# Attention steps of a conv and attention chain: scores of both images first, then the values, then the maxima tiles, on TensorE

## The chip, the cores and the metric

One Trainium2 chip, one core of it. The metric is the device time in microseconds (us) of one execution of the whole program; the median of several executions counts. TensorE (PE) multiplies, VectorE (DVE) reduces, ScalarE (ACT) takes exponentials, GpSimd (POOL) adds, SyncE (SP) issues the transfers. All five run their own list of instructions and meet only at semaphores.

## The reference

Four layers on an input of 8 images, 64 channels, 56 by 56 pixels; each layer adds its result to x. The first three (a dynamic filter, a gate, a convolution with ternary weights) are not touched by the change. The fourth is attention over all 3136 pixels of an image:

```python
def _L3_conv_ref(x, q_w, k_w, v_w):
    xf = x.reshape(b, din, hw)
    Q = jnp.einsum('kc,bcp->bkp', q_w, xf)
    K = jnp.einsum('kc,bcp->bkp', k_w, xf)
    V = jnp.einsum('vc,bcp->bvp', v_w, xf)
    S = jnp.einsum('bkp,bkq->bpq', Q, K)
    A = jax.nn.softmax(S, axis=-1)
    z = jnp.einsum('bpq,bvq->bvp', A, V)
...
x = x + _L3_conv_ref(_gn(x), L3_conv_q_w, L3_conv_k_w, L3_conv_v_w)
```

## The kernel before, in words

The images are taken in four groups of two. The two images of a group lie one above the other in the 128 partitions, and in attention each is called h (0 or 1). The first three layers of all groups run first, for 574 us; then comes attention for all groups, and it is what the change touches.

**Superblocks and steps.** Attention goes over 28 superblocks (seven per group, each 448 queries of both images), and each superblock over 25 steps j (128 keys each, the last one 64 keys). A running number k = 25 * superblock + j counts the steps. One step of PE, written out in `superblock` of the PE program, has these parts:

- `values(j)` (L1418): the exponentials of step k, in one of five slots of `Pb`, times V, added into the output bank. It is float32: four matmul records.
- `scores(k + 2, h)` (L1391): the scores of the step after the next, for image h, into the pair of PSUM banks that step k has used. So the exponentials of step k must be done before (`exp_done`). Two records for an image, one for each half of the 64-column halves of the array. The last of them releases ACT (`st_ready`).
- `max_tile` (L1353): scores again, for queries of the next superblock, whose maxima must be known before that superblock starts. 49 tiles a superblock, spread by a plan made ahead: two in nearly every step, one in step 2, and three in most steps of the first superblock up to step 17. Three PSUM banks (4, 5, 7) go round among them. Two records a tile.
- in step 2 also `denominators` (L1401, L1405) of the superblock before.

A matmul that uses 64 of the 128 columns occupies one half of the array, and each pair of records fills both halves. In step 22 (it makes the scores of the 64-key step 24) the scores of both images use the same half, so that half runs 0.38 us behind the other until the next wait that holds both. Below it is called the slow half.

**The other engines.** ACT takes the exponentials of step k (L1015) when `st_ready` says that the scores are there; then, after those of step k, it sums the exponentials of the tiles of step k - 2 that belong to the first three of seven query blocks (L980, "summed" tiles), for which it needs DVE's maxima. After the exponentials of step 0 it copies the finished output of the superblock before (`copy_output`, L1004), which waits for `pv_done`, the end of the values of step 24. DVE takes the maxima of each tile (L752) in the order in which PE makes them; in step 3 it turns the denominators (L801), between the two tiles of step 3 it inverts them (L806), between those of step 4 it turns them back (L811), after step 17 it splits the maxima in three parts (L767 to L790). Then SP sends the parts as rows into the queries (L407); `mrow_loaded` tells PE in step 23. POOL adds up the exponentials (L1145).

**What a tile waits for.** Before a tile PE waits until its bank is free (`wait_bank`): for DVE's maxima of the tile that had the bank (`max_bank_free`), or for ACT's sum (`max_scores_summed`), or, for the bank of the denominators, for DVE's transpose of them (`reciprocal_step`). By the plan the second tile of a step waits in 279 steps of the later superblocks for the second tile of the step just before, and in 308 for the first tile of it; the first tile of a step waits for something two steps back, nearly always.

**The order that is changed.** The order within a step is written by hand in the loop over j: values, then scores of image 0, a tile, scores of image 1, the other tile. Step 0 of each superblock already has the order scores, scores, values, tiles, since its values wait for `copy_output` (`ocopy`).

Of the kernel before, what the change touches and what calls it, by code (L numbers as in the profile page):

```python
# [41 lines left out]
NQ = -(-HW // QC)  # L42
# [3 lines left out]
SBS = NJ * GROUPS  # L46
# [20 lines left out]
ROW_LOADS = 4  # L67
# [99 lines left out]
def build(nc, x, weights, vectors, cst, out):  # L167
    with ExitStack() as ctx:
# [3 lines left out]
        def sem(name):  # L172
            return ctx.enter_context(nc.semaphore(name))
# [180 lines left out]
        mrow_loaded = sem("max_rows_loaded")  # L354
# [815 lines left out]
        def _(pe):  # L1170
# [176 lines left out]
            def attention():  # L1347

                def tile_of(bank, target, b, t):

                    g, s = divmod(target, NJ)
                    for h in range(2):
                        last = mm(PS[C * h:C * h + C, bank, 0:CH],  # L1353
                                  Qs[g % 2][0:KROWS, h, s * CH + b * C:s * CH + b * C + C],
                                  Ks[g % 2][0:KROWS, h, t * CH:(t + 1) * CH], start=True, stop=True)
                    return last

                def wait_rows(g):
                    pe.wait_ge(k_loaded, 16 * SPREADS * (g + 1))
                    pe.wait_ge(q_loaded, 16 * SPREADS * (g + 1))  # L1360

                def wait_bank(last):

                    what, count = last
                    if what == "reduced":
                        pe.wait_ge(mx_free, count)
                    elif what == "summed":
                        pe.wait_ge(mx_summed, count)
                    elif what == "transposed":
                        pe.wait_ge(rstep, count)  # L1370

                def max_tile(target, i, _, __, bank, last):
                    if i == 0 and target % NJ == 0:
                        wait_rows(target // NJ)
                    wait_bank(last)
                    tile_of(bank, target, *ORDER[i]).then_inc(mx_ready, 1)
# [9 lines left out]
                def scores(k, h):  # L1386

                    j = k % NQ
                    g, s = divmod(k // NQ, NJ)
                    for c in range(0, key_rows(j), C):  # L1390
                        ins = mm(PS[c:c + C, 2 * (k % 2) + h, 0:CH], Ks[g % 2][0:KROWS + 3, h, j * QC + c:j * QC + c + C],  # L1391
                                 Qs[g % 2][0:KROWS + 3, h, s * CH:(s + 1) * CH], start=True, stop=True)
                    if h == 1:
                        ins.then_inc(st_ready, 1)

                def denominators(sidx, bank):

                    pe.wait_ge(dcol_ready, sidx + 1)
                    for b in range(ACT_BLOCKS):
                        for h in range(2):  # L1400
                            mm(PS[C * h:C * h + C, bank, b * C:(b + 1) * C], dcol[:, b:b + 1].to_broadcast([P, C]),  # L1401
                               identf[:, C * h:C * h + C], start=True, stop=True)
                    pe.wait_ge(psum_pool, POOL_SUMS * (sidx + 2))
                    for h in range(2):
                        last = mm(PS[C * h:C * h + C, bank, REST:CH], ones[:, :], accP[:, h, REST:CH], start=True, stop=True)  # L1405
                    last.then_inc(d_ready, 1)

                def superblock(sidx):

                    V = Vs[sidx // NJ % 2]  # L1410

                    def values(j):
                        if j == 0:
                            pe.wait_ge(ocopy, sidx + 1)
                            if sidx % NJ == 0:
                                pe.wait_ge(v_loaded, 16 * (sidx // NJ + 1))
                        for h in range(2):
                            last = mm(PS[C * h:C * h + C, OB, 0:CH], V[:, j, C * h:C * h + C],  # L1418
                                      Pb[:, j % PSLOTS, h, :], start=(j == 0), stop=(j == NQ - 1))
                        last.then_inc(pv_done, 1)  # L1420

                    for j in range(NQ):
                        k = NQ * sidx + j
                        tiles = list(TILES_AT.get(k, ()))
                        pe.wait_ge(exp_done, k + 1)
                        if j:
                            values(j)
                        for h in range(2):
                            if k + 2 < NQ * SBS:
                                if j == NQ - 2 and h == 0:  # L1430
                                    pe.wait_ge(mrow_loaded, 16 * ROW_LOADS * (sidx + 1))
                                scores(k + 2, h)
                            if tiles and j:
                                max_tile(*tiles.pop(0))
                        if not j:
                            values(j)
                        for tile in tiles:
                            max_tile(*tile)
                        if j == FINISH_STEP - 1 and sidx:
                            bank, last = DEN_BANK.get(sidx - 1, (7, ("nothing", 0)))  # L1440
                            wait_bank(last)
                            denominators(sidx - 1, bank)
# [22 lines left out]
                for sidx in range(SBS):  # L1465
                    superblock(sidx)
# [82 lines left out]
```

## Time and profile before

| | us |
|---|---|
| median of 3 runs | 1672.35 |
| lowest and highest | 1670.41 and 1673.25 |
| the profiled execution, its own time | 1674.61 |
| its span, first to last instruction | 1672.8 |
| PE busy in the span | 1611.8 (96%) |
| ACT busy | 1194.7 (71%) |
| DVE busy | 1210.8 (72%) |
| POOL busy | 1111.8 (66%) |
| chain that ended last: share of PE | 83% |

The profiled execution spends 1.8 us outside its span. Shares over the whole span mix the first three layers with attention. In a row of the timeline the first number is the start in us from the start of the span, the second the duration in us from the first start to the last end of the merged records; "PEld" is the loading of weights, which runs beside the matmuls. A merged row of values with x4 and 0.92 us covers 0.75 us of PE, since the record of a matmul is longer than the time after which the next can start.

### The profile page before, as it was taken

The page shows a single profiled execution, that of the slowest core. Times are in us where ns is not written, and L with a number is a line of the kernel's source. Part 1 is how long each engine was busy: PE and PEld are TensorE (multiplying, and loading weights), DVE is VectorE, ACT ScalarE, POOL GpSimd, SP SyncE. Part 2 cuts the span into 40 slices and gives each one's busy share as a digit, 9 for nine tenths or more (in the row PEclk, how much of TensorE's full clock was granted, in tenths as well). Part 3 has the DMA queues.
Part 4 walks back from the last instruction along what each step waited for, and adds up shares of the span by engine and source line. Part 5 has one row for each costly group of instructions (what it writes and reads, how often), then busy time and mean ns, then how long its engine had stood idle before and what let it go on. Part 6 is the DMA issues. An engine that isn't in the chain of part 4 may idle for free.

```text
span 1672.8 us, 29841 instructions
## 1 busy us (share of the span) xinstructions
PE 1611.8 (96%) x11035; PEld 865.6 (52%) x11035; DVE 1210.8 (72%) x2322; ACT 1194.7 (71%) x2276; POOL 1111.8 (66%) x886
## 2 busy tenths in 40 slices
PE   5999999999999899999999999999999999999996
PEld 4457457557556245555555555555555555555542
DVE  5865865865955787777777777777777777777750
ACT  2053143144243689999999999999999999999984
POOL 1720730630632168888888888888888888888887
PEclk9999999999999699999999999999999999999998
DMA  2000210210205303200000500000320000000000
GB/s 96 2 38 39 69 39 39 69 39 39 69 7 103 134 2 57 65 14 17 12 13 12 110 13 18 13 12 13 52 69 12 18 12 13 12 7 7 7 7 12
DMA packets 15586, 57.68 MB, mean 34 GB/s; under 512 B 4688, under 2 KB 10960, under 8 KB 13008
## 3 DMA queue, kind: packets, MB, share of 16 engines
q1 hardware_dynamic: 15440, 55.77, 12.5%
q8 instruction: 86, 1.41, 0.3%
q14 instruction: 60, 0.49, 0.1%
HBM read 31.41 MB, written 24.22 MB: 33 GB/s over the span
## 4 chain that ended last, share of the span: by engine, by line
PE 83%; DVE 8%; POOL 5%; issue 2%; ACT 2%; DMA 0%; POOLq 0%; DVEq 0%; ACTq 0%
PE PS L1418 29%; PE PS L1353 15%; PE PS L1391 14%; PE PS L1289 7%; PE PS L1244 5%; PE PS L1232 3%; POOL accP L1145 2%; DVE nmt L752 2%; PE PS L1341 1%; PE PS L1333 1%; DVE nmt L759 1%; PE PS L1279 1%; PE PS L1278 1%; PE PS L1198 1%; DVE st L507 1%
## 5 line engine op out<-in xcount | busy, mean ns | idle before, releaser
L752 DVE TENSOR_REDUCE nmt<-PS 128x1 f32<-128x448 f32 x1323 | 767.2, 617 | 223.2 <-PE PS L1353 222.6
L1145 POOL TENSOR_TENSOR accP<-accP,Pb 128x512 f32<-128x512 f32 (+1 forms) x532 | 674.5, 1268 | 93.5 <-ACT Pb L1015 37.9
L1015 ACT ACTIVATE Pb<-PS 128x896 f32<-128x896 f32 (+1 forms) x700 | 637.0, 915 | 80.1 <-PE PS L1391 69.8
L980 ACT ACTIVATE PS<-PS,nmt 128x448 f32<-128x448 f32 x588 | 356.4, 606 | 16.4 <-DVE nmt L759 9.6
L1418 PE MATMUL PS<-Pb,VT 128*64 128x448 f32 x1400 | 335.9, 541 | 1.9 <-ACT Pb L1015 1.5
L1418 PE MATMUL PS<-Pb,xnf 128*64 128x448 f32 x1400 | 336.4, 540 | 0.0
L1353 PE MATMUL PS<-xnp,xin 96*64 96x448 bf16 x1408 | 265.4, 371 | 7.9 <-ACT PS L980 3.6
L1353 PE MATMUL PS<-Ka,Qa 96*64 96x448 bf16 x1372 | 258.8, 353 | 0.9
L1391 PE MATMUL PS<-xin,xnp 99*64 99x448 bf16 x1372 | 256.3, 353 | 0.8 <-ACT Pb L1015 0.6
L1391 PE MATMUL PS<-Qa,Ka 99*64 99x448 bf16 x1372 | 251.8, 353 | 0.0
L1353 PEld LDWEIGHTS PS<-xnp,xin 96*64 96x64 bf16 x1408 | 87.7, 113 | 138.5 <-issue 61.9
L1353 PEld LDWEIGHTS PS<-Ka,Qa 96*64 96x64 bf16 x1372 | 86.7, 110 | 117.7 <-issue 66.3
L1391 PEld LDWEIGHTS PS<-Qa,Ka 99*64 99x64 bf16 x1372 | 87.5, 109 | 113.0 <-issue 86.4
L1391 PEld LDWEIGHTS PS<-xin,xnp 99*64 99x64 bf16 x1372 | 87.2, 109 | 108.3 <-issue 78.6
L1418 PEld LDWEIGHTS PS<-Pb,VT 128*64 128x64 f32 x1400 | 101.4, 137 | 49.1 <-ACT Pb L1015 14.1
L1418 PEld LDWEIGHTS PS<-Pb,xnf 128*64 128x64 f32 x1400 | 104.5, 137 | 39.9 <-ACT Pb L1015 2.9
L980 ACT ACTIVATION_READ_ACCUMULATOR PS<-PS,nmt 128x1 f32 x588 | 117.1, 199 | 0.0
L1145 POOL TENSOR_TENSOR accQ<-accQ,Pb 128x512 f32<-128x512 f32 x84 | 106.7, 1271 | 13.7 <-ACT Pb L1015 1.9
L614 DVE SCALAR_TENSOR_TENSOR Pb<-PS,cf,xnp 128x896 f32<-128x896 f32 (+1 forms) x80 | 79.3, 1029 | 22.1 <-PE PS L1232 21.5
L1138 POOL TENSOR_TENSOR accQ<-Pb 128x512 f32<-128x512 f32 x28 | 35.6, 1271 | 87.3 <-ACT Pb L1015 87.3
L880 ACT ACTIVATE xnp<-xw,nb,rstd 128x448 f32<-128x448 f32 x28 | 19.9, 751 | 93.5 <-DVE nb L522 93.5
L1244 PE MATMUL PS<-Pb,cs 128*128 128x448 f32 x168 | 76.5, 573 | 9.3 <-DVE xw L627 9.3
(160 smaller groups left out, 1810.0 us busy)
## 6 DMA issues: line engine op xcount, KB each, us to landing
saved_v<-VT SPq DMA_DIRECT2D x4, 1600.0 KB, 11.3
xin<-in_x SPq DMA_DIRECT2D x4, 1568.0 KB, 6.5
saved_x<-xw SPq DMA_DIRECT2D x4, 1568.0 KB, 5.6
out<-xw SPq DMA_DIRECT2D x28, 224.0 KB, 1.9
saved_parts<-parts SPq DMA_DIRECT2D x4, 1176.0 KB, 8.0
xw<-saved_x SPq DMA_DIRECT2D x21, 224.0 KB, 2.6
xnf<-saved_v SPq DMA_DIRECT2D x2, 1600.0 KB, 16.6
VT<-saved_v SPq DMA_DIRECT2D x2, 1600.0 KB, 18.3
```

The source lines that it names most:

```text
L614: nc.vector.scalar_tensor_tensor(out=prod[t][:, 0:m, :].rearrange("p h (r w) -> p h r w", w=W), in0=PS[:, b:b + m, 0:CH].rearrange("p h (r ...
L752: nc.vector.reduce_max(nmt[:, target % 2, b, t:t + 1], PS[0:BLK, bank, 0:CH], X, negate=True).then_inc(mx_free, 1)
L980: return nc.scalar.activation(PS[0:BLK, bank, 0:CH], PS[0:BLK, bank, 0:CH], ACT.Exp, bias=nmt[:, target % 2, b, t:t + 1], accum_out=sm[:, ...
L1015: nc.scalar.activation(Pb[0:r, j % PSLOTS, :, :], PS[0:r, 2 * (k % 2):2 * (k % 2) + 2, 0:CH], ACT.Exp).then_inc(exp_done, 1)
L1138: nc.gpsimd.tensor_tensor(accQ[:, :, REST:CH], Pb[:, 0, :, REST:CH], Pb[:, 1, :, REST:CH], ALU.add).then_inc(psum_pool, 2)
L1145: nc.gpsimd.tensor_tensor((accQ if j < TO_ACCP else accP)[0:r, :, REST:CH], (accQ if j <= TO_ACCP else accP)[0:r, :, REST:CH], Pb[0:r, j % ...
L1232: last = mm(PS[:, 2 * ((TAPS * u + t) % TAP_SLOTS) + i, 0:CH], selb[:, t, :], SF[:, j * CH:(j + 1) * CH], start=True, stop=True)
L1244: last = mm(PS[:, ACCB + i, 0:CH], identf, prod[t][:, i, :], start=(t == 0), stop=(t == TAPS - 1))
L1289: last = mm(PS[:, CONV_BANKS[j % 5], 0:CH], wt[:, t * P:(t + 1) * P], pad_rows_at(src, j * (ROWS * PW) + (t // 3) * PW + t % 3, ROWS), sta ...
L1353: last = mm(PS[C * h:C * h + C, bank, 0:CH], Qs[g % 2][0:KROWS, h, s * CH + b * C:s * CH + b * C + C], Ks[g % 2][0:KROWS, h, t * CH:(t + 1 ...
L1391: ins = mm(PS[c:c + C, 2 * (k % 2) + h, 0:CH], Ks[g % 2][0:KROWS + 3, h, j * QC + c:j * QC + c + C], Qs[g % 2][0:KROWS + 3, h, s * CH:(s + ...
L1418: last = mm(PS[C * h:C * h + C, OB, 0:CH], V[:, j, C * h:C * h + C], Pb[:, j % PSLOTS, h, :], start=(j == 0), stop=(j == NQ - 1))
```

## The change: what it does

In the steps 1 to 24 of a superblock PE's list is put in another order; step 0 stays as it was. Scores of image 0 and of image 1 come first, one behind the other, then the values, then all tiles of the step. Two waits move with this: that for `exp_done` stays first in the step but now stands before the scores, and that for the maxima rows (`mrow_loaded`, step 23) now stands before the values and not behind them. Nothing is added and nothing is removed; the lists of ACT, DVE, POOL and SP are the same as before.

```diff
                         pe.wait_ge(exp_done, k + 1)
-                        if j:
-                            values(j)
-                        for h in range(2):
-                            if k + 2 < NQ * SBS:
-                                if j == NQ - 2 and h == 0:
-                                    pe.wait_ge(mrow_loaded, 16 * ROW_LOADS * (sidx + 1))
+                        if k + 2 < NQ * SBS:
+                            if j == NQ - 2:
+                                pe.wait_ge(mrow_loaded, 16 * ROW_LOADS * (sidx + 1))
+                            for h in range(2):
                                 scores(k + 2, h)
-                            if tiles and j:
-                                max_tile(*tiles.pop(0))
-                        if not j:
-                            values(j)
+                        values(j)
                         for tile in tiles:
                             max_tile(*tile)
```

PE's list before, at the turn from one superblock to the next: step 24, then step 0 up to its values. L1418 are values, L1391 scores, L1353 tiles; one row of values or tiles is one image.

```order
L1418 MATMUL PS<-Pb,VT 64x448 [waits exp_done]
L1418 MATMUL PS<-Pb,VT 64x448
L1391 MATMUL PS<-Qa,Ka 64x448 x2
L1353 MATMUL PS<-Ka,Qa 64x448 [waits max_scores_summed]
L1353 MATMUL PS<-Ka,Qa 64x448
L1391 MATMUL PS<-Qa,Ka 64x448 x2
L1353 MATMUL PS<-Ka,Qa 64x448 [waits max_bank_free]
L1353 MATMUL PS<-Ka,Qa 64x448
L1391 MATMUL PS<-Qa,Ka 64x448 [waits exp_done]
L1391 MATMUL PS<-Qa,Ka 64x448 x3
L1418 MATMUL PS<-Pb,VT 64x448 [waits output_copied]
```

The same place of PE's list in the changed kernel.

```order
L1391 MATMUL PS<-Qa,Ka 64x448 [waits exp_done]
L1391 MATMUL PS<-Qa,Ka 64x448 x3
L1418 MATMUL PS<-Pb,VT 64x448 x2
L1353 MATMUL PS<-Ka,Qa 64x448 [waits max_scores_summed]
L1353 MATMUL PS<-Ka,Qa 64x448
L1353 MATMUL PS<-Ka,Qa 64x448 [waits max_bank_free]
L1353 MATMUL PS<-Ka,Qa 64x448
L1391 MATMUL PS<-Qa,Ka 64x448 [waits exp_done]
L1391 MATMUL PS<-Qa,Ka 64x448 x3
L1418 MATMUL PS<-Pb,VT 64x448 [waits output_copied]
```

In step 24 the values, on whose end `copy_output` waits, moved behind the four score matmuls; step 0 is as before. The second place is step 5 of PE's list before, whose first tile takes the bank of the denominators and whose second waits for the second tile of step 4.

```order
L1418 MATMUL PS<-Pb,VT 64x448 [waits exp_done]
L1418 MATMUL PS<-Pb,VT 64x448
L1391 MATMUL PS<-Qa,Ka 64x448 x2
L1353 MATMUL PS<-Ka,Qa 64x448 [waits reciprocal_step]
L1353 MATMUL PS<-Ka,Qa 64x448
L1391 MATMUL PS<-Qa,Ka 64x448 x2
L1353 MATMUL PS<-Ka,Qa 64x448 [waits max_bank_free]
```

And in the changed kernel.

```order
L1391 MATMUL PS<-Qa,Ka 64x448 [waits exp_done]
L1391 MATMUL PS<-Qa,Ka 64x448 x3
L1418 MATMUL PS<-Pb,VT 64x448 x2
L1353 MATMUL PS<-Ka,Qa 64x448 [waits reciprocal_step]
L1353 MATMUL PS<-Ka,Qa 64x448
L1353 MATMUL PS<-Ka,Qa 64x448 [waits max_bank_free]
```

The first tile has moved behind the scores of image 1, next to the second tile; the second has the same place, counted from the start of the step.

## Rows read from the trace of the kernel before

**Rows 1.** Superblocks: stretch, us, busy PE PEld DVE ACT POOL (count), PEclk, DMA.

```profile
574.20:619.20 45.00, 42.54 (x325) 19.01 (x322) 36.06 (x70) 39.46 (x82) 30.58 (x25) 1.00 0.00 1
...
968.88:1007.70 38.82, 38.75 (x315) 19.76 (x313) 30.29 (x61) 36.12 (x72) 32.80 (x27) 1.00 0.04 13
...
1626.40:1672.80 46.40, 33.31 (x228) 12.11 (x224) 3.25 (x7) 23.77 (x30) 37.56 (x32) 0.89 0.03 10
```

**Rows 2.** Waits from 700 to 1600 us: total us, times, longest.

```profile
ACT Pb L1015 <- PE PS L1391: 55.2, 117, 0.6
PEld PS L1353 <- DVE nmt L752: 44.0, 165, 0.5
```

**Rows 3.** Timeline of one ordinary step: PE, and DVE's maxima.

```profile
1104.48 0.92 PE L1418 MATMUL PS<-Pb,VT 128*64 128x448 f32 x4
...
1105.23 0.35 PE L1391 MATMUL PS<-Qa,Ka 99*64 99x448 bf16 x2
...
1105.42 0.35 PE L1353 MATMUL PS<-xnp,xin 96*64 96x448 bf16 x2
...
1105.82 1.16 DVE L752 TENSOR_REDUCE nmt<-PS 128x1 f32<-128x448 f32 x2 [0.36 <-PE PS L1353]
...
1106.00 0.92 PE L1418 MATMUL PS<-Pb,VT 128*64 128x448 f32 x4
```

**Rows 4.** Timeline of a turn of superblocks: ACT from 967.42.

```profile
967.42 0.91 ACT L1015 ACTIVATE Pb<-PS 128x896 f32<-128x896 f32 x1
968.28 0.54 ACT L1004 ACTIVATE Osb<-PS 128x448 f32<-128x448 f32 x1
...
969.33 0.92 ACT L1015 ACTIVATE Pb<-PS 128x896 f32<-128x896 f32 x1
```

**Rows 5.** The same turn, PE: values of step 24, of step 0, tiles, next weights.

```profile
967.68 0.54 PE L1418 MATMUL PS<-Pb,VT 128*64 128x448 f32 x1
...
969.21 0.92 PE L1418 MATMUL PS<-Pb,VT 128*64 128x448 f32 x3
...
970.30 0.20 PEld L1418 LDWEIGHTS PS<-Pb,VT 128*64 128x64 f32 x4 [0.22 <-ACT Pb L1015]
```

**Rows 6.** PE in step 0, a narrower stretch: two tiles on one half.

```profile
969.68 0.55 PE L1353 MATMUL PS<-Ka,Qa 96*64 96x448 bf16 x2
```

**Rows 7.** Timeline of steps 4 and 5: DVE, then PE.

```profile
976.84 0.62 DVE L752 TENSOR_REDUCE nmt<-PS 128x1 f32<-128x448 f32 x1 [0.27 <-PE PS L1353]
977.38 0.64 DVE L811 STREAM_TRANSPOSE RF<-Rc 128x448 f32<-128x448 f32 x1
977.94 0.58 DVE L752 TENSOR_REDUCE nmt<-PS 128x1 f32<-128x448 f32 x1
```

**Rows 8.** The same, PE.

```profile
977.02 0.92 PE L1418 MATMUL PS<-Pb,VT 128*64 128x448 f32 x4
...
978.58 0.11 PEld L1353 LDWEIGHTS PS<-Ka,Qa 96*64 96x64 bf16 x2 [0.50 <-DVE nmt L752]
...
978.80 0.92 PE L1418 MATMUL PS<-Pb,VT 128*64 128x448 f32 x4
```

**Rows 9.** Timeline of steps 18 and 19: DVE's last maximum of step 18, the waiting tile.

```profile
999.08 0.61 DVE L752 TENSOR_REDUCE nmt<-PS 128x1 f32<-128x448 f32 x1
...
999.74 0.11 PEld L1353 LDWEIGHTS PS<-Ka,Qa 96*64 96x64 bf16 x2
...
999.89 0.36 PE L1353 MATMUL PS<-Ka,Qa 96*64 96x448 bf16 x2
```

**Rows 10.** Timeline of steps 21 to 23: last issue of maxima rows, values of step 23.

```profile
963.55 0.70 SPq L407 DMA_DIRECT2D Qa<-mpt  x1
...
965.79 0.92 PE L1418 MATMUL PS<-Pb,VT 128*64 128x448 f32 x3
```

**Rows 11.** The page's DMA issues: count, KB each, us from issue to landing.

```profile
out<-xw SPq DMA_DIRECT2D x28, 224.0 KB, 1.9
...
xw<-saved_x SPq DMA_DIRECT2D x21, 224.0 KB, 2.6
```

## The prediction

> **What bounds the kernel now.** I read the busy times by superblock first, then the waits, then the timeline. In the middle superblocks PE is busy for 38.75 of 38.82 us, at the full clock, while DVE has 30.3, ACT 36.1 and POOL 32.8 us of work [rows 1]. The row of waits has ACT waiting for PE's scores for 55.2 us between 700 and 1600 us [rows 2]; that is what the change could shorten, but it is idle time of an engine that is not the bound. The timeline says how full PE is. Values take 1105.23 - 1104.48 = 0.75 us, a pair of score or tile matmuls 1105.42 - 1105.23 = 0.19, and the step 1106.00 - 1104.48 = 1.52 [rows 3], which is 0.75 plus four pairs of 0.19 with nothing left over. So the reader is to see two things: nearly every step has no gap, and there the order can win nothing; and the places where PE does wait decide the sum. Busy PE hides them, since the record of a matmul (0.35) is longer than its pace (0.19).
>
> Three kinds of such places exist before. In step 5 of every superblock the second tile waits for DVE. Its weights load 0.50 us late at 978.58, and the next values start at 978.80 where 977.02 + 1.52 = 978.54 was due: 0.26 us [rows 8]. The first superblock has three tiles in most steps; it takes 45.0 us where 38.8 and 14 more tiles of 0.19 make 41.5, so it loses 3.5 [rows 1]. The last superblock has no tiles and belongs to POOL, 37.56 us busy to PE's 33.31 [rows 1]; the order of PE's work does not move its end.
>
> **The change, part by part.** PE's work is the same. Each switch costs what it did, since two adjacent tiles, which the changed kernel has in every step, already stand in step 0: two records in 0.55 us, that is starts 0.55 - 0.35 = 0.20 apart [rows 6]. The cost of the switches is nothing.
>
> Counted from the start of a step, the scores end 0.94 us earlier (0.75 + 0.19), so ACT may start earlier. The values end 0.38 later. The first tile comes 0.19 later, at 1.14 instead of 0.95, and the second stays at 1.33. DVE starts 0.40 after a step's first tile and takes 1.16 for both (1105.42, 1105.82) [rows 3], so both maxima are done 0.19 us later in the step. That is what costs.
>
> *Ordinary step.* DVE would end at 1105.62 + 0.40 + 1.16 = 1107.18 and release the weights 0.06 later, at 1107.24, as 978.52 to 978.58 [rows 7, 8]. The second tile of the next step is due at 1104.48 + 1.52 + 1.33 = 1107.33. Hidden by 0.09; if the 0.11 us load [rows 9] cannot run beside its matmul, 0.01 or 0.02 show, in at most 279 steps: 0 to 4 us. I take 0, since at 978.58 the load starts and the values follow 0.22 later, only 0.03 more than a tile [rows 8].
>
> *Step 5.* DVE takes the first maxima of step 4 at 976.84, turns the reciprocals back at 977.38, and takes the second from 977.94 to 978.52 [rows 7]. All of it hangs on the first tile, 0.19 later now, while the waiting tile of step 5 is due at the same time as before. The loss goes from 0.26 to 0.45: +0.19 (a part of it may already fall in step 4, behind the inversion between the tiles of step 3; the sum is the same).
>
> *Step 19.* The maxima of step 18 are delayed by the splitting, end at 999.08 + 0.61 = 999.69, and release the load at 999.74; its tile starts at 999.89 on time [rows 9]. With 0.19 more the load is released at 999.93, 0.02 is lost to it as above, and the tile runs at 999.96: +0.07.
>
> *Turn of a superblock.* This is the largest term. ACT copies the output after the exponentials of step 0, once the values of step 24 are done: they end on the slow half at 967.68 + 0.54 = 968.22 [rows 5] and the copy starts at 968.28 [rows 4]. Behind it on ACT stand the sum of a tile and the exponentials of step 1, which start 969.33 - 968.28 = 1.05 after the copy and end at 970.24 [rows 4]; the weights for step 1 load at 970.30 [rows 5]. The slow half of PE is due for step 1 at 969.21 + 0.75 + 0.38 = 970.34 [rows 5], so nothing is lost before. After the change the values of step 24 stand behind the scores of both images, 0.38 later. Copy, sum and exponentials all move by 0.38: release at 970.68, and PE, whose work up to there is the same, is due at 970.34. Lost: 0.35 (0.34 and a late load's 0.02). Copying is the wait that the early scores don't help: ACT reaches it no later than 968.28 in both kernels, since the exponentials before it, 967.42 + 0.91 = 968.33 [rows 4], overlap its start and have some 0.15 to spare even if the maxima before them come 0.19 later.
>
> *Row transfer.* PE's wait for the rows of maxima in step 23 moves ahead of the values, 0.75 earlier, and the rows leave 0.19 later. The last is issued at 963.55 [rows 10]; its landing has no row. The nearest are 1.9 and 2.6 us, for far larger transfers [rows 11]: 963.55 + 0.19 + 1.9 = 965.64 or 966.34, against 965.79 for the start of step 23 [rows 10]. So 0 or 0.6 us a superblock. I take 0, since 21 rows of 32 bfloat16 numbers are small and nearer to the quick one; the upper bound would be 26 * 0.6 = 16 us.
>
> *First superblock.* With three tiles a step DVE's third maximum also ends about 0.2 later, and in about eight of these steps a tile waits for it or for its sum: +1.5 us, between -3.5 (early exponentials let ACT sum sooner and all the loss goes) and +3.
>
> **Sum.** 26 superblocks with tiles before and after their turn: 26 * (0.35 + 0.19 + 0.07) = 26 * 0.61 = 15.9 us, and 1.5 for the first: +17.4. Nothing stands on the side of the gains, because ACT's earlier start meets DVE's later maxima. The profiled execution would go from 1674.6 to 1692.0 us; it stands 2.3 above the median, so the median goes from 1672.35 to 1689.8. A difference of 0.2% is 3.3 us, about what a measurement can tell.
>
> **A rule of the skill against the rows.** Two adjacent tiles start 0.20 us apart with their loads hidden [rows 6]. By the Trainium skill, "TensorE: Matmul & The Clock Gate", section "The mechanism", weights load beside a running matmul only when their row groups differ. As a mechanism of this kernel that would expose the load of 0.11 us [rows 9] at each of the two new neighbours of like shape in some 620 steps: 620 * 2 * 0.11 = 136 us, 1809 us. Rows 6 speak against it, so it has one chance in a hundred; by that rule the pairs of step 0 would start 0.30 apart, and the trace does not agree.
>
> **The rivals.** *(a) Only the tiles' waits count.* If ACT catches up at the turn (the copy is taken early, or the tile behind it is short), 26 * 0.26 = 6.8 us remain: 1679. For it speaks ACT's slack of 2.7 us in a superblock [rows 1]; against it, that the copy starts 0.06 after the values end, so it is bound by them.
>
> *(b) The transfer of the rows comes late too.* If it lands after 2.6 us, 16 us come on top: 1705. It decides from a landing of 2.05 us on.
>
> *(c) Faster.* ACT no longer waits for scores, so a tile that waits for ACT's sum gets its bank sooner. The place is the first superblock, the only one where such waits hold PE; it gives back up to 3.5 us there, 1668.9. It decides if ACT's wait for scores, and not DVE, sets those sums, and if the terms above are hidden by exponentials that come early. For it speaks the 55.2 us [rows 2]; against it, that step 5, in which DVE alone holds PE, can only get worse.
>
> *(d) No difference.* PE's pace covers the new waits as it covers the old ones: 1672. It needs the copy not to hang on step 24, against rows 4 and 5.
>
> **Chances.** The forecast 0.60 (1689.8), (a) 0.18, (b) 0.08, (c) 0.06, (d) 0.07, the rule 0.01. Slower by over 0.2%: 0.60 + 0.18 + 0.08 + 0.01 = 0.87; within 0.2%: 0.07; faster: 0.06. The range takes in (a) and the upper ends of ordinary step and first superblock (1689.8 + 4 + 1.5, and part of a late transfer): 1678 to 1698; (b), (c), (d) and the rule, 0.22 together, lie outside it or at its edge.
>
> **What the changed profile would show.** A middle superblock of 39.4 us instead of 38.8. Before the scores of step 1 a wait of PE for ACT of 0.3 us or more, 26 times, and the copy 0.38 later in its step. The second tile of step 5 waiting for DVE some 0.7 us, that of step 19 for 0.2. ACT's wait for scores gone from the list, its waits for DVE new. In steps 6 to 17 a pace of 1.52 still. No wait in step 23. I am wrong if ordinary steps stretch to 1.55 (the 0.09 were not there), if step 1 starts on time, or if the first superblock takes under 45.

## The result: slower by one per cent, and where the time shows

The median rises from 1671.79 us (four runs, 1670.41 to 1673.25) to 1688.2 us (four runs, 1686.83 to 1689.11). The ratio is 1.0097, with a 95% interval from 1.008 to 1.0115. The profiled execution of the changed kernel took 1687.33 us, its span is 1685.5 us; before they were 1674.61 and 1672.8.

I read the superblocks first. Columns are those of [rows 1]. In the view of busy times by stretch, each line runs from the last of the four value matmuls of step 0 in one superblock, which is on PE's slow half, to the same matmul of the next. Below are the first superblock and a middle one, of before and then of after. (These stretches start at another matmul than those of [rows 1], so the edges differ a little; both kernels are cut in the same way here.)

```profile
574.54:619.91 45.37, 42.91 (x328) 19.42 (x325) 36.77 (x71) 39.83 (x83) 30.58 (x25) 1.00 0.00 1
...
969.59:1008.44 38.85, 38.78 (x315) 19.79 (x313) 30.32 (x61) 36.16 (x72) 32.80 (x27) 1.00 0.04 13
```

```profile
572.98:619.52 46.54, 42.29 (x328) 19.36 (x324) 36.69 (x71) 39.14 (x82) 30.54 (x25) 1.00 0.00 1
...
973.91:1013.28 39.37, 39.05 (x315) 18.85 (x312) 30.33 (x61) 36.00 (x73) 32.81 (x27) 1.00 0.04 13
```

The number of instructions and the work of DVE, ACT and POOL did not change. The middle superblock grew by 0.52 us, the first by 1.17 here (1.45 if it is cut at the first of the four matmuls). Over the superblocks 2 to 25 the mean went from 38.85 to 39.36, so +0.50. From the start of attention to the end of the span it is 1685.5 - 572.98 = 1112.5 us against 1672.8 - 574.54 = 1098.3: +14.3. In this pair of executions the changed kernel reached attention 1.6 us earlier, with the same instructions in front of it. Over all the traces of this study attention starts between 570.0 and 575.1 us, whatever its order is, so the length of a superblock is the cleaner measure, and the medians carry some 2 us of this (more on it at the sum below).

The waits between 700 and 1600 us of the changed kernel (total us, times, longest):

```profile
PEld PS L1353 <- DVE nmt L752: 116.7, 319, 0.9
ACT PS L980 <- DVE nmt L752: 58.2, 160, 0.5
...
ACT Pb L1015 <- PE PS L1391: 11.2, 23, 0.5
PEld PS L1391 <- ACT Pb L1015: 10.9, 22, 0.5
PEld PS L1418 <- ACT Osb L1004: 7.0, 22, 0.3
```

ACT's wait for scores fell from 55.2 us [rows 2] to 11.2, and 58.2 us of waiting for the maxima came in its place: ACT is no further ahead, it only stands before another door. PE's weight loads for tiles wait 116.7 us for DVE, where it was 44.0 [rows 2]. Most of that is idle time of the loader which no matmul feels, as the ordinary step shows: lines of its timeline (start, us, engine, line, operation; in brackets the idle time ahead of it and its releaser).

```profile
993.02 0.92 PE L1418 MATMUL PS<-Pb,VT 128*64 128x448 f32 x4
...
993.87 0.11 PEld L1353 LDWEIGHTS PS<-Ka,Qa 96*64 96x64 bf16 x2 [0.36 <-DVE nmt L752]
...
994.54 0.54 PE L1418 MATMUL PS<-Pb,VT 128*64 128x448 f32 x2
```

The weights of the second tile are released at 993.87, 0.09 before its matmul is due (values 0.75 and one tile 0.19 after 993.02 make 993.96), and the next step starts 994.54 - 993.02 = 1.52 later. What answers to [rows 7] and [rows 8], the steps 4 and 5, is the first place where the wait is felt:

```profile
981.60 0.62 DVE L752 TENSOR_REDUCE nmt<-PS 128x1 f32<-128x448 f32 x1 [0.27 <-PE PS L1353]
...
981.98 0.92 PE L1418 MATMUL PS<-Pb,VT 128*64 128x448 f32 x4
...
982.14 0.63 DVE L811 STREAM_TRANSPOSE RF<-Rc 128x448 f32<-128x448 f32 x1
...
982.70 1.69 DVE L752 TENSOR_REDUCE nmt<-PS 128x1 f32<-128x448 f32 x3
982.73 0.36 PE L1353 MATMUL PS<-Ka,Qa 96*64 96x448 bf16 x2
...
983.33 0.11 PEld L1353 LDWEIGHTS PS<-Ka,Qa 96*64 96x64 bf16 x2 [0.86 <-DVE nmt L752]
983.34 0.38 PE L1353 MATMUL PS<-Ka,Qa 96*64 96x448 bf16 x2 [0.24 <-DVE nmt L752]
...
983.93 0.54 PE L1418 MATMUL PS<-Pb,VT 128*64 128x448 f32 x2
```

`turn_back` stands between the two maxima of step 4. The second tile of step 5, due at 982.73 + 0.19 = 982.92, starts at 983.34, and the values come 983.93 - 981.98 = 1.95 after those before: 0.43 late, where it was 0.26. The second place is the turn. ACT first (it answers to [rows 4]), then PE [rows 5]:

```profile
971.85 0.91 ACT L1015 ACTIVATE Pb<-PS 128x896 f32<-128x896 f32 x1
972.88 0.54 ACT L1004 ACTIVATE Osb<-PS 128x448 f32<-128x448 f32 x1
...
973.93 0.92 ACT L1015 ACTIVATE Pb<-PS 128x896 f32<-128x896 f32 x1
```

```profile
973.48 0.20 PEld L1418 LDWEIGHTS PS<-Pb,VT 128*64 128x64 f32 x4 [0.32 <-ACT Osb L1004]
...
974.90 0.14 PEld L1391 LDWEIGHTS PS<-Qa,Ka 99*64 99x64 bf16 x4 [0.50 <-ACT Pb L1015]
```

The copy starts 1.03 after the exponentials of step 0, where it was 0.86 (the exponentials last 0.91, so ACT now stands idle; they are themselves about 0.19 later in the step than before), and PE waits twice: the values of step 0 for the copy, some 0.10 in all, and the scores of step 1 for the exponentials, from which it gets free at 974.90, 0.23 late.

The third place is small. The second tile of step 19 waits for the maxima of step 18, which the splitting delays:

```profile
1003.97 0.61 DVE L752 TENSOR_REDUCE nmt<-PS 128x1 f32<-128x448 f32 x1
...
1004.63 0.11 PEld L1353 LDWEIGHTS PS<-Ka,Qa 96*64 96x64 bf16 x2 [0.51 <-DVE nmt L752]
...
1005.23 0.54 PE L1418 MATMUL PS<-Pb,VT 128*64 128x448 f32 x2
```

Counted from the values at 1003.63, the next come 1.60 later instead of 1.52. The table gathers the steps of all superblocks 2 to 25. A step is measured from the last of its four value matmuls to that of the next, and the means of both kernels are worked out from the starts in the timeline.

| piece of a superblock | before | after | difference |
|---|---|---|---|
| steps 24, 0 and 1 together | 4.569 | 4.906 | +0.34 |
| steps 4 and 5 together | 3.295 | 3.487 | +0.19 |
| step 19 | 1.520 | 1.601 | +0.08 |
| each ordinary step (some 19) | 1.520 | 1.514 | -0.006 |
| superblock | 38.853 | 39.356 | +0.50 |

The pieces add to 0.34 + 0.19 + 0.08 - 19 * 0.006 = 0.50.

### The profile page after: what moved, and what is told of

It reads as the page before. It is cut to its first block, busy times and chain, and to the rows that moved or that the text cites. A ratio compares the mean times of both kernels' runs of the same rounds, so it can differ in the third digit from the quotient of the medians.

```text
span 1685.5 us, 29868 instructions
## 1 busy us (share of the span) xinstructions
PE 1615.9 (96%) x11035; PEld 843.8 (50%) x11035; DVE 1211.1 (72%) x2322; ACT 1189.9 (71%) x2276; POOL 1112.2 (66%) x886
## 4 chain that ended last, share of the span: by engine, by line
PE 81%; DVE 8%; POOL 4%; ACT 4%; issue 2%; DMA 0%; SPq 0%; POOLq 0%; ACTq 0%; DVEq 0%
PE PS L1418 28%; PE PS L1391 14%; PE PS L1353 14%; PE PS L1289 7%; PE PS L1244 5%; PE PS L1232 3%; DVE nmt L752 3%; POOL accP L1145 2%; PE PS L1341 1%; PE PS L1333 1%; ACT Pb L1015 1%; DVE nmt L759 1%; PE PS L1279 1%; PE PS L1278 1%; PE PS L1198 1%
## 5 line engine op out<-in xcount | busy, mean ns | idle before, releaser
L1015 ACT ACTIVATE Pb<-PS 128x896 f32<-128x896 f32 (+1 forms) x700 | 628.5, 912 | 23.5 <-PE PS L1391 17.7
L1418 PE MATMUL PS<-Pb,VT 128*64 128x448 f32 x1400 | 333.7, 540 | 0.8 <-ACT Pb L1015 0.4
L1418 PE MATMUL PS<-Pb,xnf 128*64 128x448 f32 x1400 | 333.5, 540 | 0.0
L1353 PE MATMUL PS<-xnp,xin 96*64 96x448 bf16 x1408 | 215.6, 372 | 11.9 <-DVE nmt L752 4.9
L1353 PE MATMUL PS<-Ka,Qa 96*64 96x448 bf16 x1372 | 203.8, 353 | 3.4 <-DVE nmt L752 3.4
L1391 PE MATMUL PS<-Qa,Ka 99*64 99x448 bf16 x1372 | 200.8, 353 | 2.5 <-ACT Pb L1015 0.6
L1391 PE MATMUL PS<-xin,xnp 99*64 99x448 bf16 x1372 | 200.2, 353 | 1.7 <-ACT Pb L1015 0.6
L1353 PEld LDWEIGHTS PS<-xnp,xin 96*64 96x64 bf16 x1408 | 85.3, 112 | 200.7 <-issue 86.5
L1353 PEld LDWEIGHTS PS<-Ka,Qa 96*64 96x64 bf16 x1372 | 83.9, 108 | 187.5 <-issue 96.0
L1418 PEld LDWEIGHTS PS<-Pb,VT 128*64 128x64 f32 x1400 | 102.8, 136 | 47.3 <-ACT Osb L1004 4.8
L1418 PEld LDWEIGHTS PS<-Pb,xnf 128*64 128x64 f32 x1400 | 103.0, 136 | 44.9 <-ACT Osb L1004 4.1
L1391 PEld LDWEIGHTS PS<-Qa,Ka 99*64 99x64 bf16 x1372 | 79.3, 109 | 63.4 <-ACT Pb L1015 17.5
L1391 PEld LDWEIGHTS PS<-xin,xnp 99*64 99x64 bf16 x1372 | 79.8, 109 | 50.1 <-ACT Pb L1015 7.5
L1087 POOL TENSOR_TENSOR Qa<-Pb 128x896 f32<-128x896 f32 (+1 forms) x16 | 29.6, 1849 | 85.5 <-DVE Pb L614 85.2
```

The costliest lines, as they stand in the source:

```text
L1015: nc.scalar.activation(Pb[0:r, j % PSLOTS, :, :], PS[0:r, 2 * (k % 2):2 * (k % 2) + 2, 0:CH], ACT.Exp).then_inc(exp_done, 1)
L1353: last = mm(PS[C * h:C * h + C, bank, 0:CH], Qs[g % 2][0:KROWS, h, s * CH + b * C:s * CH + b * C + C], Ks[g % 2][0:KROWS, h, t * CH:(t + 1 ...
```

## Experiments

The theory: three waits cost the time, each because one thing was moved later in the step. The copy hangs on the values of step 24 (turn), the maxima of step 4 on the first tile (step 5), those of step 18 likewise (step 19). The rivals are that early scores and late values also do something in ordinary steps, that ACT and not DVE holds step 5, or that a turn costs something by its adjacent pairs and not by the copy. Below a ratio is that to the kernel before, with its 95% interval; "superblock" is the mean of 2 to 25, 38.85 before and 39.36 after.

**e1: only the turn.** The kernel before, in which step 24 alone has the new order.

```diff
-                        if j:
+                        late = j in (0, NQ - 1)
+                        if not late:
                             values(j)
...
-                            if tiles and j:
+                            if tiles and not late:
                                 max_tile(*tiles.pop(0))
-                        if not j:
+                        if late:
                             values(j)
```

> The kernel before with one step of 25 in the changed order: only step 24 takes both scores, then the values, then the tiles. Theory (the output copy waits for the values of step 24, and behind it on ACT stand a tile sum and the exponentials of step 1): the copy 0.38 us later in its step, PE waiting 0.35 us before step 1 in 26 superblocks, +9.1 us, a median 9 us above the kernel before on the same chip. Rival (the cost is that of the tiles' banks in all the other steps): within 1 us of before.

Measured: 1684.41 against 1672.42 us, ratio 1.0068 (1.0056 to 1.008). Superblock 39.23, which is 0.38 more, and the first superblock as before (45.46). The superblocks make 26 * 0.38 = 9.9 of the 12.0 us between the medians; the rest is no more than what lies ahead of attention differs by. Moving the values behind four score matmuls in this one step costs about what the prediction gave the turn. ACT at the turn of this kernel:

```profile
969.55 0.91 ACT L1015 ACTIVATE Pb<-PS 128x896 f32<-128x896 f32 x1
970.78 0.54 ACT L1004 ACTIVATE Osb<-PS 128x448 f32<-128x448 f32 x1 [0.32 <-PE PS L1418]
...
971.83 1.73 ACT L1015 ACTIVATE Pb<-PS 128x896 f32<-128x896 f32 x2
```

The copy starts 1.23 after the exponentials, and the trace names the values of step 24 as what it waited for.

**e2: all but the turn.** The changed kernel, with step 24 in the old order (the edit is shown against the kernel before).

```diff
-                        if j:
+                        new = j != NQ - 1
+                        if not new:
                             values(j)
...
-                            if tiles and j:
+                            if tiles and not new:
                                 max_tile(*tiles.pop(0))
-                        if not j:
+                        if new:
                             values(j)
```

> The changed kernel with step 24 put back in the order of before. Theory: the turn costs nothing again, 26 * 0.35 = 9.1 us less than the changed kernel, so some 7 us above before (1679); superblocks of 39.0 us instead of 39.35; step 5 and step 19 still wait as in the changed kernel. Rival (ACT is late at the turn for other reasons, such as the later maxima): it stays near the changed kernel, +16 us on before.

Measured: 1680.01 us, ratio 1.0046 (1.0033 to 1.0058), superblock 39.11. So it gives back 0.24 a superblock and not 0.35: with step 24 as before the turn still costs some 0.10 (the steps 23, 24, 0 and 1 together take 6.19 us, before 6.09). The reason is on ACT:

```profile
966.89 0.61 ACT L980 ACTIVATE PS<-PS,nmt 128x448 f32<-128x448 f32 x1 [0.51 <-DVE nmt L752]
...
967.52 0.90 ACT L1015 ACTIVATE Pb<-PS 64x896 f32<-64x896 f32 x1
968.41 0.61 ACT L980 ACTIVATE PS<-PS,nmt 128x448 f32<-128x448 f32 x1
...
969.03 0.91 ACT L1015 ACTIVATE Pb<-PS 128x896 f32<-128x896 f32 x1
969.83 0.54 ACT L1004 ACTIVATE Osb<-PS 128x448 f32<-128x448 f32 x1
```

ACT stood idle until the late maxima came at 966.89 and has been without a gap since. The copy starts 0.80 after the exponentials, right behind them; the values of step 24 had ended by then (on PE, 968.72 + 0.92 = 969.64), and the copy could have started 0.06 later, at 969.70. 969.83 - 969.70 = 0.13, and most of this is the rest of the loss. Two things delay the copy in the changed kernel, late values (0.38) and late exponentials (0.19), and only the later of them shows. The two halves of the change do not add up: e1 costs 0.38, taking it out again gives 0.24.

**e3: only the tiles late.** The kernel before, values first, scores of both images next, both tiles last.

```diff
                                 scores(k + 2, h)
-                            if tiles and j:
-                                max_tile(*tiles.pop(0))
                         if not j:
```

> The kernel before with one part of the change: values stay first, but both scores stand together and the first tile behind them, so that a step reads values, scores, scores, tiles. Only the first tile moves, 0.19 us later. Theory: DVE's maxima end 0.19 later; steps 4 and 5 lose 0.19 more, step 19 0.08, the first superblock 1.5 us: 26 * 0.27 + 1.5 = +8.5 us on before, no wait for ACT at step 1. Rival (the cost comes from values that end later): the same as before within 1 us.

Measured: 1681.34 us, ratio 1.0051 (1.0039 to 1.0063), superblock 39.14. Step 5 is 1.95 us, step 19 is 1.60, as in the changed kernel, and the first superblock is 46.43, also as there (46.54). So the steps 5 and 19 and the first superblock lose by the first tile's 0.19, and the place of the values is nothing to them. The turn loses 0.13 here too (steps 23, 24, 0 and 1: 6.22), although the values of step 24 did not move: it is the part of the late tiles that e2 showed.

**e4: the changed kernel with `turn_back` later.** In DVE's list it goes behind the second tile of step 4, so that this tile's maxima don't wait for it.

```diff
-                        if j == FINISH_STEP + 1 and sidx:
-                            turn_back(sidx - 1)
                         if j == SPLIT_STEP + 1 and sidx < SBS - 1:
...
                             between(j)
+                        if j == FINISH_STEP + 1 and sidx:
+                            turn_back(sidx - 1)
```

> The changed kernel, with DVE's turning back of the reciprocals (0.64 us) behind the second tile of step 4 and no longer between its two tiles. Theory (the wait of PE in step 5 is DVE's: that transpose delays the maxima on which the tile of step 5 waits): the maxima of step 4 end 0.54 earlier, the 0.44 us lost in steps 4 and 5 go, up to 0.06 shows in step 6: 26 * 0.4 = 10 us less than the changed kernel, about +6 on before. Rival (the first tile of step 5 waits for the denominators' bank, or ACT holds it): unchanged, +16 on before.

Measured: 1675.76 us, ratio 1.0021 (1.0013 to 1.003), superblock 38.92: 0.44 less than the changed kernel, and step 5 at 1.51 has no gap left. DVE held step 5, and nothing else did.

**e5: the same edit in the kernel before.**

> The kernel before, its PE order untouched, with DVE's turning back of the reciprocals behind the second tile of step 4. Theory: PE's only regular wait of before, 0.26 us in step 5, goes; superblocks of 38.59 instead of 38.85 us, 26 * 0.26 = -6.7 us (1665). Rival (other waits move into its place, as the later transpose delays DVE into step 5): at most -2 us.

Measured: 1665.49 us (1663.24 to 1667.5) against 1672.65, ratio 0.9959 (0.9946 to 0.9971); superblock 38.59. This beats both kernels. Its middle superblock, and DVE and PE in the steps 4 and 5:

```profile
964.78:1003.37 38.59, 38.59 (x315) 20.02 (x313) 30.29 (x61) 36.05 (x72) 32.86 (x27) 1.00 0.04 14
```

```profile
972.03 1.16 DVE L752 TENSOR_REDUCE nmt<-PS 128x1 f32<-128x448 f32 x2 [0.27 <-PE PS L1353]
...
972.21 0.92 PE L1418 MATMUL PS<-Pb,VT 128*64 128x448 f32 x4
...
973.10 0.64 DVE L811 STREAM_TRANSPOSE RF<-Rc 128x448 f32<-128x448 f32 x1
...
973.73 0.92 PE L1418 MATMUL PS<-Pb,VT 128*64 128x448 f32 x4
```

Both maxima run without a gap, the transposition follows, and the next values come after 1.52. PE is busy for 38.59 of 38.59 us.

**e6: the values behind both pairs of scores and tiles** in the steps 1 to 23, with scores and tiles alternating as before. It separates "the tiles are late" from "the scores are early".

```diff
-                        if j:
+                        late = 0 < j < NQ - 1
+                        if j and not late:
                             values(j)
...
-                        if not j:
+                        if late or not j:
                             values(j)
```

> The other way to bring the scores early: steps 1 to 23 read scores, tile, scores, tile, values; steps 0 and 24 as in the kernel before. The scores end 0.57 us earlier in the step than in before, the first tile 0.75 earlier, and the tiles keep their distance of 0.38. Theory (early scores are worth nothing, since PE has no gap; what costs is the copy behind step 24 and the late first tile, and here neither is late): the same as before within 3 us, step 5 still 0.26 late. Rival (early scores help by themselves, masked in the changed kernel): 3 us or more faster than before.

Measured: 1689.01 us, ratio 1.0102 (1.0088 to 1.0116), superblock 39.52: as slow as the changed kernel, where both the theory and its rival had said no slower than 3 us above the kernel before. Every ordinary step takes 1.520; all of the loss, 0.67, lies between the steps 0 and 1:

```profile
975.25 0.82 PE L1353 MATMUL PS<-Ka,Qa 96*64 96x448 bf16 x4
...
975.93 1.69 DVE L752 TENSOR_REDUCE nmt<-PS 128x1 f32<-128x448 f32 x3 [0.55 <-PE PS L1353]
...
977.14 0.11 PEld L1353 LDWEIGHTS PS<-Ka,Qa 96*64 96x64 bf16 x2 [0.92 <-DVE nmt L752]
```

Step 0 has its tiles last and step 1 now has them first, so that DVE gets four tiles within about 1 us, and needs 1.69 for three of them. The fourth was due some 0.67 earlier, and its bank is free at 977.14 only. What counts for DVE is the distance from tile to tile across the border of two steps, not the place within one. The first superblock takes 44.90 us here and in e7, where it took 45.37 before: this is the one place where work that comes earlier gained something, 0.5 us in the whole kernel.

**e7: e6 with `turn_back` later.**

> e6 with the turning back of the reciprocals behind the second tile of step 4. Theory: another -6.7 us against e6, so 1665 to 1668. Rival (in this order DVE has no wait of PE to give back): as e6.

Measured: 1681.86 us, ratio 1.0058 (1.0045 to 1.0071), superblock 39.26, which is 0.26 less than e6. The gain of e5 stands in this order too, 7.2 us between the medians, as it should if DVE alone holds step 5; the level of 1665 to 1668 that was expected rested on an e6 as fast as the kernel before.

**e8: tiles ahead of the scores.** Values, both tiles, both scores in the steps 1 to 24, with `turn_back` later.

```diff
                         pe.wait_ge(exp_done, k + 1)
+                        if j:
+                            values(j)
+                            for tile in tiles:
+                                max_tile(*tile)
+                            tiles = []
                         if k + 2 < NQ * SBS:
...
-                        values(j)
+                        if not j:
+                            values(j)
```

> Steps 1 to 24 read values, tiles, scores, scores, with the turning back behind the second tile of step 4. The first tile is 0.19 earlier than in before, the scores end 0.19 later, values as in before. Theory (late first tile and late values cost, late scores do not, since ACT has 2.7 us to spare in a superblock; like neighbours together run a step in 1.514 instead of 1.520, as seen in the changed kernel): superblocks of 38.45 to 38.6, 8 to 10 us below before (1662 to 1665). Rival (ACT needs the scores early; then the changed order had a gain on that side): waits of PE for ACT in many steps, no faster than before.

Measured: 1687.08 us, ratio 1.0083 (1.0069 to 1.0097): a miss by over 20 us. Superblock 39.03, and the first superblock takes 55.15 instead of 45.37. Of it the line of busy times, the loader's and ACT's timeline:

```profile
572.32:627.47 55.15, 43.96 (x328) 19.46 (x326) 38.09 (x71) 39.59 (x83) 30.56 (x25) 1.00 0.00 1
```

```profile
601.49 0.14 PEld L1353 LDWEIGHTS PS<-xnp,xin 96*64 96x64 bf16 x4 [1.30 <-ACT PS L980]
```

```profile
599.90 0.92 ACT L1015 ACTIVATE Pb<-PS 128x896 f32<-128x896 f32 x1 [0.89 <-PE PS L1391]
600.72 0.60 ACT L980 ACTIVATE PS<-PS,nmt 128x448 f32<-128x448 f32 x1
...
602.48 0.92 ACT L1015 ACTIVATE Pb<-PS 128x896 f32<-128x896 f32 x1 [1.04 <-PE PS L1391]
```

This is a circle. A tile needs the bank that ACT frees by its sum (ends 601.43, load at 601.49). The scores stand behind that tile on PE. ACT has nothing to do until these scores come (1.04 us idle), and its next sum stands behind their exponentials. A step costs 602.48 - 599.90 = 2.58 us. In the kernel before, and in the changed one, the scores stand ahead of the tile which waits for ACT, and that is what this part of the order is good for. In later superblocks, with two tiles a step, it shows in the steps 1 (1.76) and 3 (1.71) only. Step 19 takes 1.60 us as in e3, although its first tile stands 0.19 earlier here than in the kernel before and not later: e3 and e8 have in common that the two tiles of a step stand 0.19 apart and not 0.38, so it is this distance that costs.

**e9: e7 with step 0 in the same order too.** The condition of e6 becomes `late = j < NQ - 1`, and a tile follows its scores in step 0 as well. It should take the pile of four tiles away.

> e7 with step 0 in the order of steps 1 to 23 (scores, tile, scores, tile, values); step 24 stays values first. e6 and e7 lost 0.67 us between step 0 and step 1, where the tiles of step 0 stand late and those of step 1 early, so that four tiles come to DVE within 1 us. Theory (that pile of tiles is their whole loss, early scores themselves neither cost nor help): superblocks of 38.6 to 38.7 instead of e7's 39.26, -16 us against e7, 1666 to 1668. Rival (the values last in the steps hold ACT's copy or the slots of the exponentials): as e7, 1682.

Measured: 1675.75 against 1673.21 us, ratio 1.0019 (1.0008 to 1.0029), superblock 39.08. Half a miss: DVE's pile is gone, another wait stands in its place.

```profile
969.30 0.54 ACT L1004 ACTIVATE Osb<-PS 128x448 f32<-128x448 f32 x1 [0.69 <-PE PS L1418]
...
970.52 0.11 PEld L1353 LDWEIGHTS PS<-Ka,Qa 96*64 96x64 bf16 x2 [0.74 <-ACT PS L980]
```

The first tile of step 0 comes early now, and its bank is freed by a sum which stands on ACT behind the copy. The copy is late itself: ACT stands idle for 0.69 us until the values of step 24 are done, so the rival, that late values hold the copy, is right in part. Against e5 0.49 us are lost in the mean. In the kernel before, where step 0 has its tiles last, no such wait holds PE.

**e10: the turn with a short sum.** e1, in which the sum of a tile behind the copy takes 8 columns of 448, so that most of this tile is missing in the denominators. If the chain values, copy, sum, exponentials is what costs, a sum that is 0.37 us shorter must give most of e1's 0.38 back.

```diff
-                def tile_sum(target, b, t, bank):
-                    return nc.scalar.activation(PS[0:BLK, bank, 0:CH], PS[0:BLK, bank, 0:CH], ACT.Exp,
+                def tile_sum(target, b, t, bank, n=CH):
+                    return nc.scalar.activation(PS[0:BLK, bank, 0:n], PS[0:BLK, bank, 0:n], ACT.Exp,
...
-                                tile_sum(target, b, t, bank).then_inc(mx_summed, 1)
+                                tile_sum(target, b, t, bank, 8 if j == 0 and sidx else CH).then_inc(mx_summed, 1)
```

> e1 (before, step 24 alone in the new order) with the tile sum that stands on ACT between the output copy and the exponentials of step 1 cut from 448 to 8 columns in superblocks 1 to 27, which leaves most of that sum out of the denominators. Theory (the chain is values of step 24, copy, sum, exponentials of step 1): these exponentials come some 0.37 earlier, the 0.38 us of e1 shrink to about 0.1, the values of step 0 waiting for the copy itself; +2.5 us on before instead of +11. Rival (the late exponentials are not behind that sum, or something else holds step 1): +9 to +11.

Measured: 1673.83 us, ratio 1.0009 (0.9999 to 1.002), superblock 38.94, which is 0.09 above the kernel before, where e1 had 0.38. In this kernel ACT reads

```profile
965.03 0.54 ACT L1004 ACTIVATE Osb<-PS 128x448 f32<-128x448 f32 x1 [0.32 <-PE PS L1418]
965.48 0.24 ACT L980 ACTIVATE PS<-PS,nmt 128x8 f32<-128x8 f32 x1
...
965.72 1.73 ACT L1015 ACTIVATE Pb<-PS 128x896 f32<-128x896 f32 x2
```

The copy is as late as in e1 (1.23 after the exponentials at 963.80), but the next exponentials follow it by 0.69 instead of 1.05. By itself the late copy costs 0.09 of the 0.38, as the values of step 0 wait for it; the rest comes from what stands behind it on ACT.

**e11: the changed kernel with both cures**, step 24 in the old order and `turn_back` later.

> The changed kernel with both places mended: step 24 back in the old order and the turning back of the reciprocals behind the second tile of step 4. Theory (the places are independent): superblocks of 39.11 - 0.44 = 38.67 us, so 26 * -0.18 + 1.1 for the first superblock = -3.6 us on before, 1668 to 1669, and 2 to 3 us above e5, which has the old order everywhere. Rival (mending one place brings out another wait): 1672 or more.

Measured: 1669.8 us, ratio 0.9982 (0.9973 to 0.9992), superblock 38.68. The changed order is then faster than the kernel before, and slower than e5 (38.59), which has the same cure of step 5 in the old order. So also with its worst two places taken away the new order wins nothing over the old: the pace gives 0.006 a step, and the rest of the turn (0.10), step 19 (0.08) and the first superblock (46.44 against 45.37) take more.

## Why the prediction was right, point by point

*What bounds the kernel* held: the work of no engine changed, and all of the time appears as gaps of PE. "Nearly every step has no gap, and there the order can win nothing" was almost right, see the pace below.

*The turn*, 0.35 forecast: 0.34 by the steps 24, 0 and 1 and 0.38 in e1 by itself. The mechanism is shown twice, by the copy that waits for the values (e1) and by the short sum that gives the loss back (e10). One sentence of this step is wrong. It said that the exponentials ahead of the copy "have some 0.15 to spare even if the maxima before them come 0.19 later". They have this against the late copy of the changed kernel, but not against the early one: e2 put the values back and the exponentials held the copy 0.13 late (e3 loses by the same). The term is right for the kernel that was predicted; its reading as one cause was not.

*Step 5*, 0.26 to 0.45, +0.19: steps 4 and 5 together +0.19. e3 shows the first tile to be the cause, e4 that `turn_back` is in the way. One reading is off, without a consequence: the 0.50 at the load of 978.58 [rows 8] is how long the loader stood idle, not how late the load was; the lateness is the 0.26 by which the next values came late. *Step 19*, +0.07: +0.08, or 0.087 over the pace of this kernel.

*First superblock*, +1.5 with a range from -3.5 to 3: +1.2 or +1.45, depending on the half at which it is cut, and e3 has it too. The waits of its loader for DVE went up from 5.7 to 9.6 us, and those for ACT's sums did not go down (5.5 and 6.0). The rival (c), that earlier sums give back the 3.5 us, is out by this.

*Ordinary step*, 0 with an upper bound of 4 us: the cover of 0.09 held (0.09 in the rows above too). The pace was to be 1.52 "still", and this missed by a little in the good direction. From the values of step 6 to those of step 17, eleven steps, before (first fence, its start is 978.80 in [rows 8]) and after (second fence, start 983.93 above):

```profile
995.52 0.92 PE L1418 MATMUL PS<-Pb,VT 128*64 128x448 f32 x4
```

```profile
1000.60 0.92 PE L1418 MATMUL PS<-Pb,VT 128*64 128x448 f32 x4
```

(995.52 - 978.80) / 11 = 1.520 and (1000.60 - 983.93) / 11 = 1.515. It is 0.006 a step, 0.12 a superblock, 3 us in the kernel. This is the term by which the sum was too large.

*Transfer of the rows*, 0: right in nearly all superblocks. The range's other end was not idle, though. In the superblocks 1 and 20 of the changed kernel step 22 took 1.77 and 1.63 us instead of 1.51, about 0.4 us in all. The weights of the scores of step 23 load there 2.40 and 2.25 us after the last rows were issued, everywhere else 1.84 to 1.88 after, and the exponentials that they wait for too were long done. That it was the rows is argued from this; no row names them.

*The sum.* Forecast +17.4 us; the medians differ by 16.4, and from the start of attention on the profiled executions differ by 14.3. By pieces it is 1.2 for the first superblock, 0.7 for superblock 1 with its late rows, 24 * 0.50 = 12.1 for those from 2 to 25, and 0.25 for the last two together (81.57 and 81.82 us), which is 14.3. So the terms gave 3 us more than there was, most of it by the pace (24 * 0.11 = 2.6).

That the forecast of 1689.8 is nearer to the median of 1688.2 than this is luck. The executions of the kernel before, in the series for the experiments, go by their mean granted clock: thirteen at 0.982 have a median of 1674.9 us, nine at 0.985 one of 1672.2, seven at 0.987 one of 1670.2. The changed kernel has two at 0.982 (1689.08 and 1689.11) and two at 0.985 (1686.83 and 1687.33). At like clock the difference is 14.2 and 14.9, which agrees with the 14.3; the other 2 us most likely come from the mix of executions in the two medians. The clock differs ahead of attention, where the change does nothing, as between 200 and 300 us of the two profiled executions (before, then after; the clock stands behind the busy times), and it is 1.00 in the middle superblocks of both.

```profile
200.00:300.00 100.00, 95.39 (x462) 63.14 (x461) 62.44 (x134) 40.47 (x67) 22.75 (x20) 0.95 0.09 33
```

```profile
200.00:300.00 100.00, 95.40 (x475) 62.62 (x475) 64.96 (x136) 40.45 (x67) 23.95 (x21) 0.98 0.10 36
```

*The rule* of the Trainium skill on loads beside a running matmul ("TensorE: Matmul & The Clock Gate", section "The mechanism") would, as the prediction applied it, have given 1809 us. The trace does not agree with it: all steps with like pairs next to each other, whose loads of 0.11 us would have shown by it, are not slower but 0.006 us faster. The 1809 rested on counting the 96 rows of a tile and the 99 rows of a score as different groups. They share most of their rows, and the loads between them are hidden in the kernel before as well (1.52 us a step is 0.75 and four times 0.19, with nothing left for a load).

*Rivals.* (a), that ACT catches up at the turn, is excluded by e1, (b) by the steps 22 and 23, which are on time in all superblocks but two, (d) by the result.

## What to carry to other kernels

Where one engine is full, as PE is here, letting others start earlier wins next to nothing (0.5 us in the best order tried); look instead for each place where that engine waits, and ask of each what stands between the wait and what releases it. Here one DVE instruction that nobody waited for stood between two that PE waited for; moving it was worth 7 us, while the reordering as a whole cost 16. And before a queue is reordered, list who waits for each item and what stands behind that waiter on its own queue: the four matmuls moved ahead of the values cost 0.38 us by way of a copy, a sum and an exponential on ACT, and in e8 a tile ahead of the scores closed a circle that cost 10 us in one superblock. Steps of unlike order meet at their borders (e6): count the distance between two consumers of one engine across the border, not within the step.

## What was not expected of the hardware

- The pace of PE depends a little on what stands next to what, with the same matmuls. Orders with like pairs adjacent in the ordinary steps (after, e2, e3, e4, e8, e11) take 1.514 us a step, those with scores and tiles alternating (before, e1, e5, e6, e7, e9, e10) 1.520, thirteen kernels without an exception. Why is open.
- A load that is released late costs little beyond its lateness. In step 5 it starts at 983.33 and its matmul's record at 983.34; the values follow 983.93 - 983.34 = 0.59 later, where the tile and two pairs of scores are due to take 3 * 0.19 = 0.57.
- A shorter ACT instruction is not shorter in proportion: the sum of 448 columns takes 0.60 us, that of 8 columns 0.24.
